# Attention's row maxima: two query tiles side by side in TensorE's row halves, reduced 1024 wide

## The reference, cut to what matters

```python
qkv = x @ qkv_w + qkv_b                       # (2048, 3 * 16 * 64)
q, k = _rope(q, k, S, D)                      # 16 heads of 64
attn = jnp.einsum('bhqd,bhkd->bhqk', q, k) / 8
attn = jax.nn.softmax(attn, axis=-1)          # over 2048 keys
out = jnp.einsum('bhqk,bhkd->bhqd', attn, v)
return out @ out_w + out_b
```

## Time and profile before

| | |
|---|---|
| median of 3 runs | 1983.98 us (1982.47 to 1987.57) |
| the profiled execution | 1981.65 us |
| its span, first to last instruction | 1979.9 us |
| mean granted TensorE clock | 0.95 |
| busy: PE, DVE, ACT, POOL | 1782.2, 1439.9, 1437.3, 1409.4 us |
| L368, maxima matmuls | 1024, mean 385 ns |
| L553, maxima reduces | 1024, mean 686 ns |

### The profile page before, as it was taken

How to read it: one execution, slowest core, us unless ns; L and a number is a source line. 1 busy time by engine, 2 the same in 40 slices (tenths; PEclk the granted TensorE clock), 3 DMA queues, 4 the chain that set the end, 5 groups by cost and what they waited for, 6 DMA issues and landing times. The chain is left out here.

```text
span 1979.9 us, 54360 instructions
## 1 busy us (share of the span) xinstructions
PE 1782.2 (90%) x23072; PEld 1109.6 (56%) x23072; DVE 1439.9 (73%) x2638; ACT 1437.3 (73%) x1755; POOL 1409.4 (71%) x797
## 2 busy tenths in 40 slices
PE   5999999999999999999999999768999999769936
PEld 1466666666666666666666666664565666333523
DVE  5787877877878778787787776148978888344764
ACT  1688888888888888888888899427988888422421
POOL 3699899899899899899899899756655666022000
PEclk8899999999999999999999999888999999768968
DMA  4101101011011010110100100411111111000000
GB/s 115 29 18 29 25 22 29 21 26 29 18 29 25 22 29 21 26 29 21 26 23 24 26 10 2 134 42 43 43 37 35 40 35 32 5 1 0 0 0 22
DMA packets 71018, 56.59 MB, mean 29 GB/s; under 512 B 29164, under 2 KB 64312, under 8 KB 70776
## 3 DMA queue, kind: packets, MB, share of 16 engines
q1 hardware_dynamic: 70776, 53.11, 10.6%
HBM read 14.21 MB, written 1.05 MB: 8 GB/s over the span
## 5 line engine op out<-in xcount | busy, mean ns | idle before, releaser
L304 POOL TENSOR_TENSOR ah_probs_lo<-ah_probs,ah_probs_hi 128x1024 f16<-128x1024 f32 x512 | 1081.1, 2133 | 130.8 <-ACT ah_probs L496 130.7
L553 DVE TENSOR_REDUCE ah_part_max<-ah_p_m 128x1 f32<-128x512 f32 x1024 | 682.7, 686 | 185.4 <-PE ah_p_m L368 170.2
L493 ACT ACTIVATE ah_probs_hi<-ah_p_s 128x1024 f16<-128x1024 f32 x512 | 524.2, 1024 | 181.7 <-PE ah_p_s L387 161.1
L496 ACT ACTIVATE ah_probs<-ah_p_s 128x1024 f32<-128x1024 f32 x512 | 521.1, 1018 | 0.0
L401 PE MATMUL ah_p_o<-ah_v_hi,ah_probs_hi 128*128 128x65 f16 x4096 | 477.0, 195 | 34.3 <-DVE a_attn L568 28.9
L405 PE MATMUL ah_p_o<-ah_v_hi,ah_probs_lo 128*128 128x65 f16 x4096 | 476.5, 194 | 0.0
L403 PE MATMUL ah_p_o<-ah_v_lo,ah_probs_hi 128*128 128x64 f16 x4096 | 476.4, 193 | 0.0
L401 PEld LDWEIGHTS ah_p_o<-ah_v_hi,ah_probs_hi 128*128 128x128 f16 x4096 | 383.3, 98 | 140.8 <-DVE a_attn L568 59.8
L403 PEld LDWEIGHTS ah_p_o<-ah_v_lo,ah_probs_hi 128*128 128x128 f16 x4096 | 378.8, 98 | 96.8
L368 PE MATMUL ah_p_m<-ah_k_hi_lo,ah_q_hi_twice 128*128 128x512 f16 x1024 | 393.4, 385 | 7.1 <-DVE ah_part_max L553 5.6
L386 PE MATMUL ah_p_s<-ah_q_hi_twice,ah_k_hi_lo 128*128 128x512 f16 x1024 | 388.8, 380 | 0.3 <-ACT ah_probs L496 0.3
(11 more groups left out here) (280 smaller groups left out, 3131.5 us busy)
## 6 DMA issues: line engine op xcount, KB each, us to landing
ba_v_skew<-ba_v_own SPq DMA_DIRECT2D x64, 129.0 KB, 2.4
ah_q_hi_twice<-ah_hi SPq DMA_DIRECT2D x128, 64.0 KB, 2.0
ah_k_hi_lo<-ah_hi SPq DMA_DIRECT2D x64, 64.0 KB, 1.9
ah_one_k_hi<-ah_hi SPq DMA_DIRECT2D x64, 64.0 KB, 2.0
ah_k_hi_lo<-ah_lo SPq DMA_DIRECT2D x64, 64.0 KB, 2.0
ah_max_q_lo<-ah_lo SPq DMA_DIRECT2D x64, 64.0 KB, 2.0
ah_w_head<-in_w_heads SPq DMA_DIRECT2D x16, 160.0 KB, 2.5
bw_rot<-in_rot SPq DMA_DIRECT2D x4, 512.0 KB, 9.9
```

Source lines behind the costliest of these rows:

```text
L304: pool.tensor_tensor(pl[:, p % RW, :, :], pb[:, p % RP, :, :], ph[:, p % RW, :, :], ALU.subtract).then_inc(lo_pool, 1)
L493: act.activation(ph[:, p % RW, :, :], p_s[:, p % 2, :, :], ACT.Exp, scale=HD ** -0.5)
L496: act.activation(pb[:, p % RP, :, :], p_s[:, p % 2, :, :], ACT.Exp, scale=HD ** -0.5).then_inc(exp_done, 1)
L553: dve.tensor_reduce(part[:, t, 2 * half + b:2 * half + b + 1], p_m[:, b, :], AX, ALU.max).then_inc(maxed, 1)
```

## The change

Each step's two maxima matmuls now stand together, behind the first half of `weigh`, and one reduce reads both banks. Before, a step took one query tile against two chunks of 512 keys, with all 128 rows: the high query part against the high and the low part of the keys. Now it takes two query tiles against one chunk of keys, each with 64 rows: the first tile from rows 0 to 63 of `qa` and `ka`, the second from rows 64 to 127 of `qa` and `kb`. Both products are of high parts alone. The number of maxima matmuls is the same, 1024; the reduces become 512 of 128x1024 with two results a partition. `maxed` counts steps instead of halves, and the matmuls of a step wait for the reduce of the step before it.

```diff
-                def maxima(q, halves=(0, 1)):
+                def maxima(q):
 
                     e, i = divmod(q, PAIRS_A)
                     n, c = divmod(e, QC)
-                    t, half = divmod(i, 2)
-                    s, rows = n % SETS, slice((c * TPC + t) * P, (c * TPC + t + 1) * P)
-                    if c == 0 and i == 0 and 0 in halves:
+                    pair, ck = divmod(i, QC)
+                    s = n % SETS
+                    if c == 0 and i == 0:
                         for b in range(2):
                             pe.wait_ge(spread[b], SPREAD * QC // 2 * (n + 1))
-                    for b in halves:
-                        if q >= 1:
-                            pe.wait_ge(maxed, 2 * q - 1 + b)
-                        pe.matmul(p_m[:, b, :], qa[:, s, rows], ka[:, s, chunk(2 * half + b)], start=True,
+                    if q >= 1:
+                        pe.wait_ge(maxed, q)
+                    for b, keys in ((0, ka), (1, kb)):
+                        half = slice(b * HD, (b + 1) * HD)
+                        first = (c * TPC + 2 * pair + b) * P
+                        pe.matmul(p_m[:, b, :], qa[half, s, first:first + P], keys[half, s, chunk(ck)], start=True,
                                   stop=True).then_inc(m_ready, 1)
...
                     scores(p)
-                    if p + LEAD_M < STEPS_A:
-                        maxima(p + LEAD_M, (0,))
                     if p >= LAG:
                         weigh(p - LAG, 0)
                     if p + LEAD_M < STEPS_A:
-                        maxima(p + LEAD_M, (1,))
+                        maxima(p + LEAD_M)
...
-                def reduce_max(q, halves=(0, 1)):
+                def reduce_max(q):
                     e, i = divmod(q, PAIRS_A)
-                    t, half = divmod(i, 2)
-                    if i == 0 and e >= 1 and 0 in halves:
+                    pair, ck = divmod(i, QC)
+                    if i == 0 and e >= 1:
                         dve.wait_ge(m_done, e)
-                    for b in halves:
-                        dve.wait_ge(m_ready, 2 * q + b + 1)
-                        dve.tensor_reduce(part[:, t, 2 * half + b:2 * half + b + 1], p_m[:, b, :], AX,
-                                          ALU.max).then_inc(maxed, 1)
+                    dve.wait_ge(m_ready, 2 * q + 2)
+                    dve.tensor_reduce(part[:, 2 * pair:2 * pair + 2, ck], p_m[:, :, :], AX, ALU.max).then_inc(maxed, 1)
 
                 def negate_max(e):
-                    dve.wait_ge(maxed, 2 * PAIRS_A * (e + 1))
+                    dve.wait_ge(maxed, PAIRS_A * (e + 1))
...
                     if p + LEAD_M < STEPS_A:
-                        reduce_max(p + LEAD_M, (0,))
+                        reduce_max(p + LEAD_M)
                     if g <= LAST_G:
...
-                    if p + LEAD_M < STEPS_A:
-                        reduce_max(p + LEAD_M, (1,))
                     if j == 3 and e + 1 < TURNS:
```

## The result

The changed kernel takes 2035.88 us (median of 4 runs, 2032.0 to 2036.45) beside 1983.22 of the kernel before: a ratio of 1.0263, 95% interval 1.0249 to 1.0276. It is slower by 2.6%; the forecast was 2021 us, 1.9%, with a range of 1996 to 2056. The span of the profiled execution grew by 54.0 us, from 1979.9 to 2033.9.

A forecast was written before the change was run, and what follows sets the result against it. TensorE was taken to bound attention, with one wait per turn for DVE. From 1981.65 us, +33 for 57 full turns, +2 for five late turns and +4.5 before the loop gave 2021 us; range 1996 to 2056.

The forecast's parts named there:

- The pair: Each attention step: two 64-row maxima matmuls run concurrently, 0.42 us with switches against 0.434; -0.11 a turn.
- The wait for o_free: Step 2 to 3: TensorE waits for DVE's multiplication that frees p_o, 1.30 us against 0.67; +0.63 a turn.
- The wait for low_v: Step 7 to 0: the projection waits for DVE's low_v, a new wait of 0.15 us a turn.
- turn_max: Step 4 to 5: turn_max follows the pair and shares one switch, -0.09 us a turn; no wait for low, no slack.
- +0.58 a turn: Sum of the terms for a full turn, 18.92 becoming 19.5 us; over 57 turns +33 us.
- Ahead of the loop: Twelve steps of maxima before the loop run in series, about 1.9 us a step against 1.40; +4.5 us.
- the late turns: Five later turns without projections: o_free wait 0.70 us for 0.03, less 0.20 a turn; +2 us in all.
- The upper end of the range: Slower bounds: switches at 0.12 everywhere +17 us; wide reduce as long as two narrow ones, up to +20 us.
- rival A: Attention's tile-shape switches are hidden and a pair costs 0.23 us; 1980 us, not slower; chance 0.13.
- B: Rival: the pair's halves stream one after the other, 0.21 us more a step, +105 us, 2126 us; chance 0.07.

The follow-up runs named there:

- both in one half: The changed kernel with both matmuls of a pair reading rows 0 to 63, so they can't run side by side: 2127.65 us, ratio 1.0743.
- shape alone: The kernel before with each maxima matmul taking 64 rows, in its old place and with its own 512-wide reduce: 2152.11 us, ratio 1.0864.

## Why the prediction was right, step by step

**The pair: concurrent, and eaten by its switches.** Right. Side by side is worth 0.21 a step (both in one half), entering and leaving costs 0.19 (shape alone). I put the pair at 0.42, and from start to start it is that. But the narrow matmuls behind it need a little more (595.46 to 595.83, 0.37, where W has 0.36), and a plain step stayed at 2.02 where my sum had 2.01. Of the -0.11 a turn about -0.02 came.

**The wait for o_free.** Right, and the largest term: predicted 1.30, measured 1.32, against 0.67. Two moves, each alone in the changed kernel, show what it hangs on: DVE's order (36 us) and the place of the pair (54 us). Only the place is new with the change; rotate_sum stood ahead of normalise before too, and moving it there gave 30 us.

**The wait for low_v.** Right in kind, 0.15 predicted, 0.20 measured, removed by moving the projection (12 us).

**turn_max.** Here the sum failed. I booked -0.09 for a shared switch of shape and no wait, "but no slack". From pair to turn_max it is 0.39 (610.06 to 610.45) against a pair's usual 0.33, because low ends at 610.39. The wait takes most of what the shared switch gives: step 5 became 0.04 shorter, not 0.09.

**The sizes.** Forecast +0.58 a turn, measured +0.77. The misses are about 0.09 from the pair, 0.05 from turn_max, 0.04 from low_v and 0.02 from o_free; all have the same sign, so none hid another. Over 57 turns they are 11 of the 15 us by which the forecast was low. Ahead of the loop a step took 1.96 and not 1.9, and the late turns 0.52 and not 0.47 more, together about 1 us. The other 3.6 lie behind attention, for which the forecast had no term.

Two numbers of the prediction are off without changing it. The upper end of the range, by its own terms 2021 + 17 + 20, is 2058 and not 2056. And rival A gives POOL 17.2 us a turn from its busy share; in the late turns of the kernel before, POOL's subtractions start 2.09 apart, which is 16.7 for eight.

**The rivals.** A (switches hidden) fell by the shape alone: with hidden switches that kernel would have taken 1984 us, and it took 2152. B (serial) fell by the pair in one row half: made serial, the changed kernel takes 2128 us, 92 more than it does.

## What to carry to other kernels

A pair in the two row halves runs in the time of one matmul, but a group of another tile shape has to be long enough to pay for two switches: here 0.21 gained against 0.19 lost. When an edit moves a producer behind other work and merges its pieces, walk through the consumer engine's queue up to the next thing that the producer waits for; the change cost 52 us though no engine had more to do. And try the order of a queue first: one operation moved past another gave 1.6% on the kernel before.

## What I had not expected of the hardware

The switch of shape between 128x128 and 64x128 costs nearly the same in both directions and whatever the widths beside it: 0.09 into the pair and 0.10 out of it, with 65-column or 512-column neighbours. The local stage shows 0.09 at either end of its group too, and 0.12 inside it. And a group of two 64-row matmuls, fully side by side, takes TensorE almost exactly as long as two full ones at this size; I had taken that for the likeliest result, but not to a hundredth of a microsecond.
